# Key projection at the end of the step, and other places for v, kx, vx, the FFN keys, the row maxima and the x1T copy

## What is computed

```python
x = _layernorm(x + _L0_attn_ref(x, ...))    # causal attention, 16 heads; q and k pass a low-rank map of rank 32
x = _layernorm(x + _L0_xattn_ref(x, ctx_1024, mask_S2_ik0, ...))
x = _layernorm(x + _L0_ffn_ref(x, L0_ffn_W_r, L0_ffn_W_k, L0_ffn_W_v, mu_r, mu_k))
# attention: scores = q_lr @ k_lr^T * scale; causal mask; softmax; y = attn @ v; y @ Wo.T + bo
# cross attention: q, k, v by wq, wk, wv; softmax over 120 rows; entries where mask is 0 set to 0; proj
# FFN: xr, xk = mixes of x and the token before; r = sigmoid(xr @ W_r)
#      k_act = relu(xk @ W_k)^2; out = r * (k_act @ W_v)
```

## Time and profile before

| | |
|---|---|
| median of 3 runs | 970.09 us (968.84 to 973.53) |
| profiled execution: its own time | 973.32 us |
| its span | 971.6 us |
| busy, share of the span | PE 94%, PE weight load 74%, DVE 74%, ACT 61%, POOL 46% |
| mean granted clock of TensorE | 0.97 |

### The profile page before, as it was taken

One profiled execution on the slowest core, in us unless ns is written; L12 is line 12 of the kernel. 1 busy time (PEld: TensorE's weight loads), 2 busy tenths in 40 slices (PEclk: granted clock), 3 DMA queues, 4 the chain that ended last, 5 costly groups with the idle time before them and its releaser, 6 DMA issues.

```text
span 971.6 us, 25805 instructions
## 1 busy us (share of the span) xinstructions
PE 918.1 (94%) x9597; PEld 723.6 (74%) x9597; DVE 715.0 (74%) x1565; ACT 590.1 (61%) x1153; POOL 450.6 (46%) x667
## 2 busy tenths in 40 slices
PE   6789999999999999999999999999999999999975
PEld 5456778778777777777778777777778777777653
DVE  3646778788788878788778877878878887867442
ACT  2125566666776666666776666666776666656643
POOL 6202354544455455544445445454445545434453
PEclk9959999999999999999999999999999999989998
DMA  8977876656677766666688877666678777611000
GB/s 221 195 146 117 149 131 111 137 129 137 129 147 150 151 117 106 136 136 133 132 143 149 150 122 123 119 133 134 129 144 148 150 134 116 110 30 31 24 12 22
DMA packets 121447, 119.73 MB, mean 123 GB/s; under 512 B 28201, under 2 KB 104811, under 8 KB 121195
## 3 DMA queue, kind: packets, MB, share of 16 engines
q1 hardware_dynamic: 121323, 118.08, 64.3%
HBM read 75.05 MB, written 42.99 MB: 121 GB/s over the span
## 4 chain that ended last, share of the span: by engine, by line
PE 80%; ACT 8%; issue 5%; DVE 4%; POOL 2%; DMA 1%; SPq 0%; ACTq 0%; POOLq 0%; DVEq 0%
PE ps_m L500 20%; PE ps_m L492 11%; PE ps_o L594 9%; PE ps_s L513 8%; PE ps_t L513 5%; PE ps_s L528 4%; PE ps_m L463 4%; PE ps_m L649 3%; PE ps_m L472 3%; ACT p L718 3%; ACT sum L735 3%; PE ps_m L680 3%; PE ps_m L666 3%; PE ps_m L480 3%; PE ps_t L528 2%
## 5 line engine op out<-in xcount | busy, mean ns | idle before, releaser
L918 DVE TENSOR_REDUCE row_max<-ps_s 128x4 f32<-128x1024 f32 (+1 forms) x192 | 233.2, 1215 | 76.7 <-PE ps_s L528 76.5
L718 ACT ACTIVATE p<-ps_t 128x1024 f32<-128x1024 f32 x192 | 196.4, 1023 | 45.2 <-PE ps_t L528 45.1
L513 PE MATMUL ps_s<-stack 48*128 48x128 f32 (+1 forms) x1024 | 109.1, 313 | 15.5 <-DVE row_max L918 6.4
L827 ACT COPY kxT<-ps_m 128x240 f32<-128x240 f32 x32 | 11.5, 358 | 169.0 <-PE ps_m L472 169.0
L513 PEld LDWEIGHTS ps_s<-stack 48*128 48x128 f32 x1024 | 73.3, 190 | 53.4 <-DVE row_max L918 20.0
L1100 POOL TENSOR_TENSOR xT_lo<-x_in,xT_hi 128x512 fp32r<-128x512 f32 x32 | 41.4, 1293 | 151.4 <-ACT xT_hi L705 151.4
L594 PE MATMUL ps_o<-p,v_pad 128*32 128x256 f32 (+1 forms) x2048 | 96.3, 329 | 0.0
L513 PE MATMUL ps_t<-stack 50*128 50x128 f32 (+1 forms) x1024 | 93.1, 281 | 1.9 <-ACT p L718 1.4
L594 PEld LDWEIGHTS ps_o<-p,v_pad 128*32 128x32 f32 x2048 | 57.4, 109 | 43.2 <-issue 21.2
L1171 POOL TENSOR_TENSOR sum<-r_tanh,x 128x512 f32<-128x512 f32 x32 | 40.9, 1279 | 83.4 <-DVE r_tanh L1039 83.4
L513 PEld LDWEIGHTS ps_t<-stack 50*128 50x128 f32 x1024 | 75.3, 192 | 5.0 <-ACT p L718 2.7
(11 more groups left out here) (167 smaller groups left out, 2715.0 us busy)
## 6 DMA issues: line engine op xcount, KB each, us to landing
stack<-parts_dram SPq DMA_DIRECT2D x384, 128.0 KB, 5.8
parts_dram<-parts SPq DMA_DIRECT2D x64, 512.0 KB, 4.8
x_in<-in_x_turned SPq DMA_DIRECT2D x32, 256.0 KB, 8.2
x_res<-in_x SPq DMA_DIRECT2D x32, 256.0 KB, 4.0
out_x<-sum SPq DMA_DIRECT2D x64, 128.0 KB, 4.7
ctxT<-in_ctx_turned SPq DMA_DIRECT2D x32, 120.0 KB, 3.7
shift_dram<-shift_turned SPq DMA_DIRECT2D x64, 16.0 KB
stack<-shift_dram SPq DMA_DIRECT2D x64, 16.0 KB
```

Source lines behind the costliest of these rows:

```text
L513: nc.tensor.matmul(target[:, at_h:at_h + width], left[b.slot][r0:r0 + rows_n, h // 2, rows_at:rows_at + P], right[b.slot][r0:r0 + rows_n, ...
L718: nc.scalar.activation(p[c][:], ps_t[:], ACT.Exp).then_inc(exp_done[c], 1)
L918: nc.vector.tensor_reduce(row_max[:, :, j0:j0 + nj, tile], ps_s[:].rearrange("p (g j w) -> p g j w", j=nj, g=2), AX_X, ALU.max) \
```

## The change

It moves work and leaves the amount of it as it is:
- PE: k goes from slot 3's place to the end of the step, behind the second half of the product with v (`PV(1)`). v goes from behind slot 1 to ahead of it. kx and vx go from the end of the step to behind slot 1 and behind s2. k3 goes from ahead of slot 5 to behind it.
- Since k now ends with the step, its parts are split, saved and loaded to `stack` in the next step (except for batch 0). On SyncE the 12 loads then stand ahead of the shift transfers and no longer behind them.
- DVE: the row maxima of slots 3, 1 and 5 go ahead of the statistics of `sum1`, the mix of `xk` and the normalisation of `a_exp`. The x1T copy comes from ACT to DVE, between the two mixes. k's low part goes to the start of the step.
- ACT: exp of slot 3 goes ahead of the x2T copy, exp 4 ahead of `xr_hi`, exp 5 ahead of relu; k's high part goes to the start of the step, the copies of v, kx and vx follow their products.
- `BANK_USERS` gets the new order, and in it k3 stands behind s2 in one bank. Some `filler` calls stand elsewhere.

```diff
         BANK_USERS = [
-            [("q", IN, v_["q_lo"]), ("x2T", FFN, a_["x2T_ready"]),
-             ("x1T", CROSS, a_["x1T_ready"]), ("s2", CROSS, a_["a_exp_done"]), ("r3", FFN, a_["r_tanh_done"]),
-             ("z2", CROSS, v_["sum2_done"]), ("vx", PROBS, a_["vx_ready"])],
-            [("z1", CROSS, v_["sum1_done"]), ("k", IN, v_["k_lo"]),
-             ("v", SCORES, a_["v_ready"]), ("k3", FFN, a_["k_relu_done"]), ("g", CROSS, a_["g_ready"]),
-             ("v3", FFN, v_["gated_done"]), ("kx", PROBS, a_["kxT_ready"])],
+            [("q", IN, v_["q_lo"]), ("x2T", FFN, a_["x2T_ready"]), ("kx", PROBS, a_["kxT_ready"]),
+             ("s2", CROSS, a_["a_exp_done"]), ("k3", FFN, a_["k_relu_done"]), ("g", CROSS, a_["g_ready"]),
+             ("z2", CROSS, v_["sum2_done"])],
+            [("z1", CROSS, v_["sum1_done"]), ("v", SCORES, a_["v_ready"]), ("x1T", CROSS, v_["x1T_ready"]),
+             ("vx", PROBS, a_["vx_ready"]), ("r3", FFN, a_["r_tanh_done"]), ("v3", FFN, v_["gated_done"]),
+             ("k", IN, v_["k_lo"])],
         ]
...
             def step(at):
                 b = Batch(at, IN)
+                if live(at - 1, IN) and at > 1:
+                    save_parts(Batch(at - 1, IN), 1, "k_lo")
...
+                if live(at - 1, IN) and at > 1:
+                    stacks(Batch(at - 1, IN))
+                if live(at, SCORES):
+                    c = Batch(at, SCORES)
                     if c.n >= RING:
                         sp.wait_ge(shift_loaded[c.slot], Batch(c.n - RING, IN).dma_count(2))
...
-                project("k", "Wk")
-                filler(4, scores_over and on[PROBS])
-                filler(12, cross_last)
-                filler(14, ffn_last)
-                slot(1)
-                if on[CROSS]:
-                    bank = bank_free(pe, "x1T", at)
-                    pe.wait_ge(a_["x1_ready"], X.n + 1)
-                    turn_tiles(bank, x1).then_inc(filled["f_x1T"], 1)
                 if on[SCORES]:
                     bank = bank_free(pe, "v", at)
                     pe.wait_ge(g_["xT_lo"], Sb.n + 1)
                     tokens_out_split(bank, xT[Sb.slot], "Wv").then_inc(filled["f_v"], 1)
...
+                slot(1)
+                if on[PROBS]:
+                    bank = bank_free(pe, "kx", at)
+                    pe.wait_ge(ctx_loaded[Pb.n % 2], (Pb.n // 2 + 1) * 16)
+                    rows_out(bank, wx_fold, ctxT[Pb.n % 2]).then_inc(filled["f_kx"], 1)
+                if on[CROSS]:
+                    bank = bank_free(pe, "x1T", at)
+                    pe.wait_ge(a_["x1_ready"], X.n + 1)
+                    turn_tiles(bank, x1).then_inc(filled["f_x1T"], 1)
...
+                if on[PROBS]:
+                    bank = bank_free(pe, "vx", at)
+                    tokens_out(bank, ctxT[Pb.n % 2], wT["Wxv"], tiles=1, rows=M).then_inc(filled["f_vx"], 1)
+                filler(4, first_scores)
+                slot(5)
                 if on[FFN]:
                     bank = bank_free(pe, "k3", at)
                     pe.wait_ge(g_["xk_lo"], F.n + 1)
                     rows_out_split(bank, "Wkf", xk).then_inc(filled["f_k3"], 1)
-                slot(5)
...
                 PV(1)
...
+                project("k", "Wk")
```

VectorE's part:

```diff
                 row_maxima(0)
+                k_bias = [cols[:, BK, a:a + 1] for a in range(KC)]
+                if live(at - 1, IN) and at > 1:
+                    split_lo(Batch(at - 1, IN), 1, "k_hi", "k_lo", k_bias, "k")
...
+                row_maxima(3)
                 if on[CROSS]:
                     stats(0, X, sum1, v_["sum1_done"])
-                row_maxima(3)
-                if on[IN]:
-                    split_lo(A, 1, "k_hi", "k_lo", [cols[:, BK, a:a + 1] for a in range(KC)], "k")
+                row_maxima(1)
                 if on[FFN]:
                     dve.wait_ge(g_["dx_done"], F.n + 1)
                     mix(xk_f32, MUK, "xk_ready")
-                row_maxima(1)
+                if on[CROSS]:
+                    dve.wait_ge(filled["f_x1T"], X.n + 1)
+                    wait(dve, filled["f_s2"], X.n)
+                    wait(dve, v_["k_act_lo"], F.n)
+                    nc.vector.tensor_copy(flat(x1T), bank_of("x1T")[:]).then_inc(v_["x1T_ready"], 1)
```

More of the change, by code:

```diff
@@ L621, in step @@
                 slot(3)
-                filler(4, not on[FFN] and not on[IN])
+                filler(4, not on[FFN] and not on[SCORES])
                 if on[FFN]:
@@ L655, in step @@
                     rows_out_split(bank, "Wkf", xk).then_inc(filled["f_k3"], 1)
-                slot(5)
-                filler(4, not on[FFN] and not on[CROSS])
                 if on[FFN]:
@@ L661, in step @@
                     tokens_out_split(bank, xr, "Wr").then_inc(filled["f_r3"], 1)
+                filler(4, not on[FFN] and not on[CROSS])
                 if on[CROSS]:
@@ L756, in step @@
                                              scale=rstd[2][:, j:j + 1]).then_inc(x3_ready[j], 1)
+                exp(3)
                 if on[FFN]:
@@ L761, in step @@
                         .then_inc(a_["x2T_ready"], 1)
-                exp(3)
-                if on[IN]:
-                    split_hi(A, 1, "k_hi", [cols[:, BK, a:a + 1] for a in range(KC)], "k")
-                if on[CROSS]:
-                    wait(act, filled["f_x1T"], X.n)
-                    normalise(0, X, x1, sum1, "x1_ready")
-                exp(1)
-                if on[FFN]:
-                    act.wait_ge(v_["xk_ready"], F.n + 1)
-                    wait(act, filled["f_k3"], F.n)
-                    nc.scalar.copy(xk[0][:], xk_f32).then_inc(a_["xk_hi"], 1)
-                if on[CROSS]:
-                    act.wait_ge(filled["f_x1T"], X.n + 1)
-                    wait(act, filled["f_s2"], X.n)
-                    wait(act, v_["k_act_lo"], F.n)
-                    nc.scalar.copy(flat(x1T), bank_of("x1T")[:]).then_inc(a_["x1T_ready"], 1)
                 if on[SCORES]:
@@ L784, in step @@
                     last.then_inc(a_["v_ready"], 1)
+                if on[CROSS]:
+                    wait(act, filled["f_x1T"], X.n)
+                    normalise(0, X, x1, sum1, "x1_ready")
+                exp(1)
+                if on[PROBS]:
+                    act.wait_ge(filled["f_kx"], Pb.n + 1)
+                    wait(act, filled["f_s2"], Pb.n - 2)
+                    nc.scalar.copy(flat(kxT[Pb.slot]), bank_of("kx")[:, 0:KC * M]).then_inc(a_["kxT_ready"], 1)
+                if on[FFN]:
+                    act.wait_ge(v_["xk_ready"], F.n + 1)
+                    wait(act, filled["f_k3"], F.n)
+                    nc.scalar.copy(xk[0][:], xk_f32).then_inc(a_["xk_hi"], 1)
+                exp(4)
                 if on[FFN]:
@@ L788, in step @@
                     nc.scalar.copy(flat(xr[0]), flat(xr_f32)).then_inc(a_["xr_hi"], 1)
-                exp(4)
+                if on[PROBS]:
+                    act.wait_ge(filled["f_vx"], Pb.n + 1)
+                    wait(act, filled["f_z2"], Pb.n - 2)
+                    nc.scalar.copy(vx[Pb.slot][:], bank_of("vx")[0:M, 0:C]).then_inc(a_["vx_ready"], 1)
                 if on[CROSS]:
@@ L798, in step @@
                     last.then_inc(a_["a_exp_done"], 1)
+                exp(5)
                 if on[FFN]:
@@ L806, in step @@
                         .then_inc(a_["k_act_ready"], 1)
-                exp(5)
+                if on[FFN]:
+                    act.wait_ge(a_["k_act_ready"], F.n + 1)
+                    wait(act, filled["f_v3"], F.n)
+                    nc.scalar.copy(flat(k_act[0]), flat(k_act_f32)).then_inc(a_["k_act_hi"], 1)
                 if on[FFN]:
@@ L812, in step @@
                         .then_inc(a_["r_tanh_done"], 1)
-                if on[FFN]:
-                    act.wait_ge(a_["k_act_ready"], F.n + 1)
-                    wait(act, filled["f_v3"], F.n)
-                    nc.scalar.copy(flat(k_act[0]), flat(k_act_f32)).then_inc(a_["k_act_hi"], 1)
                 if on[CROSS]:
@@ L1015, in step @@
                     last.then_inc(v_["a_ready"], 1)
-                row_maxima(5)
                 if on[SCORES]:
```

58 lines of the change are left out of this document (27 added, 31 removed).

## The result

Four runs of the changed kernel had a median of 1010.7 us (1006.8 to 1012.7), four of the kernel before beside them 969.5. The ratio is 1.0425 (95% interval 1.0368 to 1.0481): slower, as forecast, and 7 us above the 1004. The profiled execution took 1006.8, its span 1005.1.

A forecast was written before the change was run, and what follows sets the result against it. TensorE bounds the full steps: 26.76 + 0.45 + 1.0 + 0.35 = 28.56 us against 27.24, so 35.6 over 27 steps, less 1 for the ends. That gives 1007.9 for the profiled execution, 1004 for the median, range 973 to 1014.

The forecast's parts named there:

- Bound and floor: TensorE bounds the full steps; without its waits of 0.22 and 0.26 us a step lasts 26.76, not 27.24.
- Late x1: VectorE's sum1 statistics start at 8.15 to 8.25 of the step, not 6.88; x1's normalisation at 10.7, not 9.72.
- Wait one: TensorE waits 0.45 us ahead of the x1T transposes for ScalarE's normalisation; it was 0.26.
- Blocked mix: GpSimd's xk_lo gets between the halves of VectorE's xr mix, which takes 1.9 us, not 0.87; chance 0.56.
- Wait two: TensorE waits 1.0 us ahead of slot 5 for slot 4's row maximum, delayed by the mix of xr.
- k3: k3 on TensorE, behind s2 in its bank, waits 0.35 us for a_exp, which hangs on slot 4's maximum.
- Sum: Full step: 26.76 + 0.45 + 1.0 + 0.35 = 28.56 us, 1.3 more than 27.24; 35.6 over 27 steps.
- the ends: Start and drain of the program: -1 us, between -4 and +4, an estimate without a row of its own.
- I cost that at nothing: SyncE's 12 stack loads ahead of the shift transfers: landed by 21 of a step of 27 or more, no cost.
- The unblocked mix: Rival: the xr mix pair takes 0.87 us, slot 5 doesn't wait; step 27.6, time 979 (973 to 985); chance 0.20.
- The clock's: Rival: TensorE's granted clock falls behind waits; once in every second step adds 12 us, giving 1017; chance 0.08.
- The faster case: Rival: normalisation starts before about 10.2, mix unblocked, waits below 0.1; time 957 (950 to 965); chance 0.13.

The follow-up runs named there:

- e9: Third order (vx between v and slot 1, k3 ahead of slot 5), with a_exp's normalisation ahead of slot 5's row maximum: 961.2 us, 0.9901 of the kernel before.
- e10: e9 with the six stack loads of the q half behind the shift transfers of q's own step again: 953.6 us, 0.9839 of the kernel before.
- e1: Changed kernel with the rounding xk_hi on ScalarE behind exp of slot 4, so GpSimd asks later: 990.1 us, 1.0196 of the kernel before.
- e4: Changed kernel with the copy of x1T back on ScalarE, ahead of xk_hi: 989.2 us, 1.0180 of the kernel before.
- e5: Changed kernel with the mix of xr ahead of the copy of x1T, both on VectorE: 1006.6 us, 1.0350 of the kernel before.
- e7: Changed kernel with the statistics of sum1 back ahead of the row maximum of slot 3: 1017.5 us, 1.0455 of the kernel before.
- e11: Changed kernel with the q half's six stack loads behind the shift transfers of q's own step: 1003.8 us (three launches), 1.0352 of the kernel before.
- e3: Kernel before with one move: VectorE takes slot 3's row maximum ahead of the statistics of sum1: 1011.0 us, 1.0413 of the kernel before.

## Why the prediction was right

- **Bound and floor.** Right: 26.76 worked out, 26.83 and 26.81 reached in e9 and e10.
- **Late x1.** Right in place: statistics at 8.01 (8.15 to 8.25 forecast), normalisation 10.54 (10.7), since the order of VectorE was the one read from the code. Wait one 0.32, not 0.45: the normalisation came 0.16 earlier, and kx takes 0.99 to the next start, not 0.91.
- **Blocked mix.** Right, shown by e1, e4 and e5: 1.89 (1.9). Wait two 0.81, not 1.0: slot 5 starts at 16.13 and not at 16.35, by the chain ahead of it. The Trainium skill, page "SBUF — State Buffer", section "Who interferes with whom", says that the one that issues first holds the ports for its whole instruction. The table of all steps agrees: GpSimd waits for the half of the mix that runs (until 0.33 or 0.72 behind the start, by the ends of xk_lo less its 1.28). Who goes first when one half has ended and both want the ports is not in that sentence; here GpSimd did if it had asked during the first half.
- **Luck in it.** Blocked or unblocked is a matter of 0.1 us: the prediction had GpSimd ask 0.4 behind the mix's start, which lies inside the border measured later (0.34 to 0.44), and it was 0.33. The choice rested on rows 5, with 0.13 there, and on my rounding; the prediction said itself that the two times lie only as far apart as their error.
- **k3.** Right: 0.37 (0.35), with s_max as its holder; in e4, with the mix unblocked, it was the copy of vx.
- **Sum.** 28.37 against 28.56: waits of 1.50 and not 1.80, floor 26.87 by the same count and not 26.76. The sum treated waits one and two as separate; e7 shows that they overlap, so "removing wait one" would have been forecast wrong by 0.3 per step. 28.56 and the ends of -1 give 1007.9 for the profiled launch, which took 1006.8, but 1004.7 for the median, written as 1004.
- **What was off.** The ends. In the profiles they are +2.5 and not -1, inside -4 to +4, but that is luck in which launches were profiled; by the medians they are about +10, and this is why 1010.7 lies 7 above the forecast. The step of it is the sentence "I cost that at nothing" on the stack loads, and e11 gives it 7 us. It looked at when the loads land in a full step, not at what the queue does to the transfer behind them, nor at the short steps of the start. The 27 full steps (31.0) and the ends make up the 33.5.
- **Rivals.** The unblocked mix is e1: 27.66 per step, forecast 27.6, but 990 and not 979, since the ends are 4.5 longer and not 1 shorter, and the median is that of the profiled execution, where I had taken 3 off. The clock's is e3. The faster case would have needed the normalisation before 10.2; e7 had it there (at 9.5 of the step), and was slower still, so that case was wrong in itself: the blocked mix decides, not x1.

## What to carry to other kernels

A wait that goes away is worth what the next engine in line has as slack: read the stretch from one slot to the next on the engine that releases it, and if it has no gap, a shorter wait ahead of it is given back at its end. Where VectorE and GpSimd both read SBUF, look at who asks while a pair of instructions runs; shifting one ScalarE instruction by 1.7 us was worth 20 us here, and by the table 0.1 us would have been enough (an estimate). And when loads move ahead of a round trip in a DMA queue, cost the round trip, in the first steps above all.

## What I hadn't expected of the hardware

- The meeting of VectorE and GpSimd has a sharp border: the mix of xr took 1.89 to 1.90 when GpSimd asked 0.13 to 0.34 behind its start, and 0.87 from 0.44 on.
- From the issue of the store of a few rows to DRAM to that of its reload, 2.5 us passed with nothing or six loads ahead in the first steps (before, e11), and 5.5, 5.9 and 4.3 behind twelve loads (steps 2 to 4 of the changed kernel). In the full step from 449.41 on it was 2.5 behind twelve loads too, and 3.9 in the step ahead of it; no run says what decides.
- A wait of 1.24 us in each step of e3 cost another 1.39 from x1T to slot 4 in those nine of 27 full steps in which the granted clock fell to 0.50 behind it; waits of up to 0.98 (e7) cost nothing beside themselves.
- In e1 the two instructions of a_nrm, which read one SBUF tensor each, took 1.46 beside GpSimd's addition, which had started 0.10 ahead of them, and 0.47 in e4, where GpSimd's had nearly ended (the rows are those of VectorE at L1032).
